# A constant multiplied beside each set in the pass for the maxima of a graph network on one Trainium2 core

## The reference

```python
def segment_softmax(scores, seg, num_segments):
    smax = jax.ops.segment_max(scores, seg, num_segments=num_segments)
    sexp = jnp.exp(scores - smax[seg])
    ssum = jax.ops.segment_sum(sexp, seg, num_segments=num_segments)
    return sexp / ssum[seg]
...
att = jnp.sum(Qh * Kh, axis=-1)          # one score per edge and head, 8 heads
alpha = segment_softmax(att, row, num_nodes)
```

## Time and profile before

| what | value |
|---|---|
| runs of the kernel before | 11170.17, 11173.09, 11174.3 us; median 11173.09 |
| profiled execution | 11176.15 us |
| its span, first to last instruction | 11174.6 us |
| mean granted clock of TensorE over the span | 0.838 |
| TensorE busy | 8588.3 us, 77% of the span |
| VectorE busy | 8220.2 us, 74% |
| ScalarE busy | 4504.9 us, 40% |
| pass for the maxima | from about 3,855 to 4,446 us |

### The profile page before, as it was taken

One profiled execution on the slowest core, in us unless ns is written; L12 is line 12 of the kernel. 1 busy time (PEld: TensorE's weight loads), 2 busy tenths in 40 slices (PEclk: granted clock), 3 DMA queues, 4 the chain that ended last, 5 costly groups with the idle time before them and its releaser, 6 DMA issues. The chain is left out here.

```text
span 11174.6 us, 317325 instructions
## 1 busy us (share of the span) xinstructions
PE 8588.3 (77%) x97527; PEld 6963.3 (62%) x97675; DVE 8220.2 (74%) x17003; ACT 4504.9 (40%) x8976; POOL 1358.2 (12%) x1625
## 2 busy tenths in 40 slices
PE   6144667886888755899994888788899959949996
PEld 5132224664777644899993556433799956648886
DVE  7498777777999866666666666566788877788887
ACT  0021001112666411566663333476677746613333
POOL 0010000110000000566560000000000002200000
PEclk9855555555999855999997999899999979979998
DMA  1100000000444311333333998677455510000000
GB/s 39 13 0 11 4 4 9 11 11 25 160 162 162 123 36 33 116 125 122 123 123 119 306 311 309 226 239 237 133 145 145 145 48 5 5 3 3 3 3 13
DMA packets 617095, 1065.01 MB, mean 95 GB/s; under 512 B 132197, under 2 KB 226381, under 8 KB 617018
## 3 DMA queue, kind: packets, MB, share of 16 engines
q1 hardware_dynamic: 487514, 890.86, 25.3%
q10 hardware_dynamic: 121152, 162.43, 3.9%
q0 software_dynamic: 8352, 10.85, 0.3%
HBM read 869.33 MB, written 194.56 MB: 95 GB/s over the span
## 5 line engine op out<-in xcount | busy, mean ns | idle before, releaser
L2453 POOL TENSOR_TENSOR acc<-acc,m_sum 128x544 f32<-128x544 f32 (+1 forms) x637 | 810.4, 1272 | 1235.3 <-ACT m_sum L2420 1195.0
L2317 DVE TENSOR_TENSOR m_msg<-m_vps,m_msg 128x512 f32<-128x512 f32 (+1 forms) x637 | 427.4, 671 | 414.3 <-PE m_vps L2358 376.5
L2382 PE MATMUL m_sps<-m_msg,m_oh 128*128 128x136 f32 x4900 | 697.3, 286 | 0.0
L2572 DVE BATCH_NORM_STATS2 stats<-t_es 128x512 f32 (+1 forms) x637 | 429.2, 674 | 357.2 <-ACT t_es L2607 351.6
L2780 PE MATMUL u_sps<-u_r,u_oh 128*128 128x128 f32 x4900 | 655.9, 276 | 24.3 <-ACT u_r L2738 24.3
L1429 PE MATMUL sp_out_x<-x,sp_adj_x 128*128 128x128 f32 x4802 | 672.8, 284 | 0.0
L2585 PE MATMUL t_eps<-t_oht,p_parts 128*128 128x512 bf16 x1764 | 486.6, 381 | 237.9 <-DVE t_oht L1495 225.2
L1413 PE MATMUL sp_aps_x<-sp_ohw_x,sp_oh_x 128*128 128x128 bf16 x7350 | 537.4, 221 | 166.1 <-DVE sp_ohw_x L1380 166.0
L2022 PE MATMUL s_qps<-q_parts,s_oht 128*128 128x128 bf16 x7203 | 511.4, 220 | 199.2 <-DVE s_oht L1495 146.8
L2764 PE MATMUL u_zps<-fcs,u_a 128*128 128x128 f32 x4916 | 655.3, 276 | 6.7 <-ACT u_a L2732 6.7
L2663 PE MATMUL g_z<-g_a,fcT 128*128 128x512 f32 (+1 forms) x1274 | 596.7, 600 | 79.9 <-ACT g_a L2651 69.7
(11 more groups left out here) (587 smaller groups left out, 20571.0 us busy)
## 6 DMA issues: line engine op xcount, KB each, us to landing
u_e<-e_tiles SPq DMA_DIRECT2D x591, 256.0 KB, 2.8
e_tiles<-t_es ACTq DMA_DIRECT2D x588, 256.0 KB, 5.4
g_e<-e_tiles SPq DMA_DIRECT2D x588, 256.0 KB, 3.4
s_rows<-bucket_rows SPq DMA_DIRECT2D x148, 768.0 KB, 4.1
m_rows<-bucket_rows SPq DMA_DIRECT2D x148, 768.0 KB, 4.1
t_rows<-bucket_rows SPq DMA_DIRECT2D x148, 768.0 KB, 7.0
s_rows<-bucket_rows SPq DMA_DIRECT2D x49, 896.0 KB, 5.0
m_rows<-bucket_rows SPq DMA_DIRECT2D x49, 896.0 KB, 5.1
```

The costliest lines, as they stand in the source:

```text
L2382: last = nc.tensor.matmul(sps[x][:, at:at + M], oh[x][:, j * P:(j + 1) * P], msg[x][:, j * M:(j + 1) * M], start=True, stop=True)
L2453: nc.gpsimd.tensor_tensor(at, at, sums[x][:, 0:n * M], ALU.add).then_inc(added, 1)
L2572: nc.vector.bn_stats(stats[:, bass.ds(w * (NQ * 6) + q * 6, 6)], es[x][:, 0:B.held(q) * P]).then_inc(stat[x], 1)
```

## The change

The pass gets one more bank of PSUM, `idle`. After the fetch of each set TensorE multiplies a constant: the bfloat16 identity is loaded as weights, and 512 columns of the constant `iota_8` stream through, into that bank. Nothing reads the bank and nothing is signalled. The semaphore `used[r]`, which tells VectorE that the set is fetched, is given by the last matmul of the fetch as before, ahead of the added one.

```diff
         tps, bps, mps = ps("x_tps", GE), ps("x_bps", W), ps("x_mps", W)
+        idle = ps("x_idle", GE)
...
                         last.then_inc(used[r], 1)
+                        nc.tensor.matmul(idle[:, :], k["ident_b"][:, :], k["iota_8"][:, 0:GE], start=True, stop=True)
```

## The result

The changed kernel takes 11373.58 us (median of four runs, 11362.99 to 11379.74) against 11171.63 us for the kernel before (the three runs of the table above and a fourth, 11169.21): a ratio of 1.018, 95% interval 1.0162 to 1.0197, or 202 us more. The forecast was 211 us more.

What follows compares the result with a forecast made beforehand. Bound per window: TensorE's stretch of sets, VectorE's chain, then a DMA wait, none overlapping. 49 x (5.12 added - 0.81 wait) = 211 us on the profiled 11176.15; median forecast 11384 us, range 11312 to 11435.

Steps and rivals of the forecast that it cites:

- TensorE paces its stretch: In each window's 13 sets, 150 matmuls run without a hole in 4.16 us, so work added between sets lengthens it one for one.
- 427 ns for each, nothing for loads: Each added 512-column matmul behind a set costs 427 ns at the lower clock; its weight load is hidden and costs nothing.
- Twelve on the path, the thirteenth beside VectorE's chain: Twelve added matmuls per window lengthen the stretch by 5.12 us; the one behind the last set costs nothing on the path.
- Free comes 2.5 us ahead of the end, and the mask's wait goes: VectorE's semaphore for SyncE's loads comes earlier against the stretch's end, so the scan's 0.81 us wait per window for the mask's DMA vanishes.
- the forecast turn: One turn of the pass's window loop goes from 12.03 to 16.34 us.
- The lower clock in the stretch: TensorE's clock stays at 0.50 while it works through the sets; a rise there was a rival with chance 0.13.
- the bucket sort: Evidence for the low clock: this stage kept TensorE busy 614 of 700 us and stayed at 0.50 throughout.
- the edge stage rose only on wide matmuls without a narrow one between them: Reason for the low clock: back-to-back 512- and 128-column matmuls preceded that stage's rise; 43% of the new stretch is 8-column matmuls.
- the 2.21 us: TensorE's busy time in the edge stage, given for the 3.41 us before the clock's rise, at 0.50 too.
- A clock over 0.50 somewhere in the pass: Sign to look for in the changed kernel's profile of the pass: it would make the forecast too high.
- The higher clock is worth next to nothing to matmuls of 8 columns: In the sets, 8-column matmuls take 25 ns at the higher clock against 26.8, so the result is slower at either level.
- The 0.27 us per window: What the higher clock would save on a window's 150 small matmuls, at 1.8 ns each.

Runs made afterwards that it cites:

- w256: The changed kernel with the added matmul streaming 256 columns instead of 512; ratio 1.0066 to the kernel before, turn 13.69 us.
- w8: The changed kernel with the added matmul streaming 8 columns instead of 512; ratio 0.9997 to the kernel before, turn 12.20 us.
- last_only: The changed kernel with the added matmul behind the last set of each window alone; ratio 0.9999 to the kernel before, turn 12.11 us.
- scores_early: The kernel before, with x_att loaded once its buffer is transposed, ahead of the wait for free, then the mask ahead of x_ends; ratio 0.9954, turn 11.13 us.
- x2: The changed kernel with two added 512-column matmuls behind each set instead of one; 11463.28 us beside 11190.28 for the kernel before.
- mask_first_after: The changed kernel with SyncE issuing the mask's transfer ahead of those of x_att and x_ends; ratio 1.0187 to the kernel before, turn 16.24 us.
- gap10: The kernel before, with ten 512-column matmuls per window in TensorE's idle time behind the transposes of x_att, none between sets; ratio 0.9987, turn 12.04 us.
- x4: The changed kernel with four added 512-column matmuls behind each set instead of one; 11749.8 us, 560 more than the kernel before.
- added_again: The changed kernel as it is, run again on the chip of the early-load kernels as their reference; ratio 1.0176 to the kernel before, turn 16.24 us.
- scores_early_added: The changed kernel with the new order of loads of scores_early; ratio 1.0185 to the kernel before, turn 16.24 us.
- scores_early_gap: scores_early plus ten 512-column matmuls per window in TensorE's idle time, as in gap10; ratio 0.9962 to the kernel before, turn 11.07 us.

## Why the prediction was right

The time lay in the range, and by the forecast's own mechanism; the forecast was 10 us high. By its steps:

- **TensorE paces its stretch.** Right at the clock of the forecast. The stretch is 9.28 us, as worked out, and w256 and the changed kernel put the cost of an added column at the lower clock's rate.
- **427 ns for each, nothing for loads.** Right: sets stand 0.746 us apart, 0.424 more than the 0.322 of before, and w8 bounds load and handover at about one small matmul.
- **Twelve on the path, the thirteenth beside VectorE's chain.** Right: in last_only the 0.43 us of the thirteenth do not show, and its 0.08 us are a wait for a DMA.
- **Free comes 2.5 us ahead of the end, and the mask's wait goes.** Right: one-hot 12 is done at 4209.60 and the last set at 4211.99, 2.4 us later, and the scan waits for nothing. The size was a little off: I took the wait that the table shows, 0.81, where the pair of scores_early and the kernel before gives 0.90. A scan that follows its predecessor in the queue starts 0.08 us before that one's recorded end (4216.44 against 4215.94 + 0.58), while one that waited does not. The table counts from that recorded end, so the 0.08 us come on top of its 0.81. That is most of the 0.1 us between the forecast turn and the measured one, 5 us over the pass. The other 5 us or so lie within what executions differ by.
- **The lower clock in the stretch.** Right, with a weaker argument than it needed. That stretches now busy had stayed low, and the bucket sort too, showed only that busy time does not decide. The reason that the edge stage rose only on wide matmuls without a narrow one between them does not hold as a rule: x2 rose with twelve narrow ones between each pair. And of the earlier trace rows the 2.21 us belong to the stretch that ends at 6064.90; the one right ahead of the rise was busy throughout. Where the changed kernel stood between the rows that stayed low and the edge stage was a guess, and that it came out is in part luck. The dose shows how near it was: two wide matmuls per set raise the clock inside the stretch. A clock over 0.50 somewhere in the pass, which I had named as a sign that the forecast was too high, turned out to be none: 0.54 in the changed kernel, 0.50 in mask_first_after with the same TensorE work, and the same turn of 16.24 us in both. The brief rises fell where TensorE had nothing to fetch. The row of the pass in mask_first_after:

```profile
3864.00:4650.00 786.00, 559.33 (x8326) 353.11 (x8325) 390.31 (x873) 75.89 (x144) 0.00 (x0) 0.50 0.10 27
```

- **The higher clock is worth next to nothing to matmuls of 8 columns.** Right: 25 ns against 27 behind the rise in x2, and 4.09 us against 4.16 for the fetch of gap10. The 0.27 us per window were even too much for this fetch, since VectorE's one-hots pace it at the higher clock: it took 4.05 us at 1.00. This is why the sign of the result did not hang on the clock.

The Trainium skill (TensorE: Matmul & The Clock Gate, Part 1) ties the higher clock to sustained activity of the engine. The rows agree with it in part: x2 and x4 rose inside their stretches, at a busy share of 100%, and the changed kernel did not in its 9.28 us, at the same busy share. So the busy share that this profile shows does not say which of these stretches would rise.

## What to carry to other kernels

Before paying for a higher TensorE clock, read what the matmuls in question cost at either level. Here those of 8 columns took 27 and 25 ns, so no clock could repay the work added to raise it. The same work in idle time was free, and gave 0.06 us of a turn at best. Work put between the pieces of the engine that paces a stretch costs its full length, less whatever wait it makes redundant further down. A faster clock can also hand the pace to another engine, as to VectorE's one-hots here. And where an instruction needs two transfers, a table of waits names only the later one: moving that one alone hands the wait to the other.

## What I had not expected of the hardware

The granted clock in the records can be wrong for a long stretch. Here are two executions of the changed kernel, first the profiled one, then added_again; of each a row from 560 to 2,600 us, a stretch that holds the bucket sort, and then the costliest TensorE group of the bucket sort:

```profile
560.00:2600.00 2040.00, 1354.73 (x12032) 846.42 (x12033) 1616.73 (x3879) 277.87 (x1169) 171.26 (x381) 0.50 0.03 7
```
```profile
L1581 PE MATMUL bs_dps<-bs_srow,bs_sel 51*128 51x128 bf16 x1978 | 295.1, 304 | 14.0 <-ACT bs_srow L1615 14.0
```
```profile
560.00:2600.00 2040.00, 1354.31 (x12029) 844.99 (x12029) 1617.17 (x3881) 278.24 (x1168) 171.66 (x382) 1.00 0.03 7
```
```profile
L1581 PE MATMUL bs_dps<-bs_srow,bs_sel 51*128 51x128 bf16 x1977 | 295.3, 305 | 14.0 <-ACT bs_srow L1615 14.0
```

The clock reads 0.50 in one and 1.00 in the other, while TensorE's busy time (1354.7 and 1354.3 us) and the mean of the same matmul (304 and 305 ns) agree. A true doubling would show in 128-column matmuls, of which twelve in a row took 1.49 us at the low level in the edge stage and 0.83 at the high one. I read it as a record that lacks its first events in the second execution: the first change of the clock in the trace stands at 52.9 us in the one and at 2680.5 in the other. Why was not tried. Of the 14 profiled executions five read 1.00 in this stretch (last_only, gap10, scores_early_added, scores_early_gap and added_again) and nine 0.50. The 0.50 that the prediction took from the earlier trace rows is borne out by the same 304 ns. But the mean over a span suffers: in the kernel before the first change stands at 497.8 us, and all ahead of it reads 1.00, where the changed kernel reads 0.50 from 59.7 to 496.6. So the means of 0.838 before and 0.817 after do not say that the change lowered the clock. A clock from this column is best checked against the duration of a matmul in the same stretch.
